# x held by channel in all stages, norms as matmuls on groups of 512 tokens inside the neighbouring loops, convolutions that take both images in turn

## The reference

```python
x = x + g(n0) * einsum(a(n0), b(n0)) @ Wo + bo        # stage 0, n0 = (x - mean) / sqrt(var + eps)
x = x + tokens + sum_e combine_e * (gelu(tokens @ w1[e]) @ w2[e] + b2[e])   # stage 1, 8 experts, top 2
x = x + block_circulant_conv3x3(n2) + b               # stage 2
x = x + moe(n3, gates from graph attention on 262144 edges)                 # stage 3, 4 experts
x = x + proj(linear_attention(q, k, v) + depthwise_conv(v))                 # stage 4
x = x + moe(n5)                                       # stage 5, 8 experts, hidden size 4 times as large
x = x + dynamic_conv(n6, kernel built from the pooled n6)                   # stage 6
x = x + moe(n7)                                       # stage 7, as stage 1
def _layernorm(x, axis=-1, eps=1e-05):
    m = jnp.mean(x, axis=axis, keepdims=True)
    v = jnp.var(x, axis=axis, keepdims=True)
    return (x - m) / jnp.sqrt(v + eps)
```

## Time and profile before

| what | us |
|---|---|
| median of 3 runs | 3209.75 |
| lowest, highest | 3207.09, 3212.43 |
| the profiled execution | 3207.62 |
| its span in the trace | 3205.9 |

### The profile page before, as it was taken

How to read it: one execution, slowest core, us unless ns; L and a number is a source line. 1 busy time by engine, 2 the same in 40 slices (tenths; PEclk the granted TensorE clock), 3 DMA queues, 4 the chain that set the end, 5 groups by cost and what they waited for, 6 DMA issues and landing times.

```text
span 3205.9 us, 20219 instructions
## 1 busy us (share of the span) xinstructions
PE 1521.4 (47%) x6554; PEld 735.1 (23%) x6554; DVE 1561.3 (49%) x2668; ACT 545.2 (17%) x858; POOL 811.7 (25%) x875
## 2 busy tenths in 40 slices
PE   0011113968673000000000012869976999699969
PEld 0011111642232000000000000244464222244443
DVE  8999995365646042222222226464146555520065
ACT  0000001024211000000000002413023555310033
POOL 0000005720003747777777761000000000000000
PEclk6555555558695555555555555869965999799979
DMA  9000001000005101111111100010000000000000
GB/s 399 26 0 0 0 13 35 14 9 0 6 17 11 57 10 18 18 18 18 18 18 18 18 13 2 1 21 1 0 1 3 1 1 1 6 0 1 1 0 27
DMA packets 70842, 65.78 MB, mean 21 GB/s; under 512 B 50449, under 2 KB 64609, under 8 KB 68321
## 3 DMA queue, kind: packets, MB, share of 16 engines
q1 hardware_dynamic: 43712, 54.60, 6.0%
q0 software_dynamic: 27040, 10.02, 3.3%
HBM read 21.96 MB, written 40.50 MB: 19 GB/s over the span
## 4 chain that ended last, share of the span: by engine, by line
PE 42%; DVE 26%; POOL 20%; issue 9%; ACT 2%; DMA 1%; POOLq 0%; DVEq 0%; SPq 0%
POOL rows L1559 15%; PE bank L840 13%; DVE keys L1806 12%; PE bank L516 8%; PE bank L558 7%; POOL rows L1549 2%; POOL tok_end L1564 2%; POOL scratch_start L1541 2%; PE bank L540 2%; DVE n_tok L396 1%; DVE mean L394 1%; PE bank L503 1%; DVE var L403 1%; PE bank L479 1%; DVE n_tok L413 1%
## 5 line engine op out<-in xcount | busy, mean ns | idle before, releaser
L1559 POOL DMA_INDIRECT rows<-scratch_row,idx_ring x512 | 485.8, 949 | 188.8 <-issue 155.7
L750 DVE TENSOR_TENSOR hid<-hid,bank 128x512 f32<-128x512 f32 (+1 forms) x320 | 273.9, 898 | 282.2 <-PE bank L540 281.5
L1222 PE MATMUL bank<-ident,last 128*20 128x128 f32 x3 | 0.8, 409 | 853.2 <-DVEq L1420 853.2
L1806 DVE TENSOR_TENSOR keys<-keys 128x1024 f32<-128x1024 f32 (+1 forms) x388 | 353.6, 953 | 7.5
L516 PE MATMUL bank<-n_chan,weights_odd 64*128 64x512 f32 x896 | 279.0, 710 | 106.6 <-ACT hid L627 106.0
L627 ACT ACTIVATE hid<-bank,weights_odd 128x512 f32<-128x512 f32 x448 | 282.9, 684 | 253.9 <-PE bank L516 253.5
L1678 POOL DMA_INDIRECT keys<-scratch_sorted,weights_odd x128 | 125.3, 979 | 537.4 <-DVEq L1859 495.8
L558 PE MATMUL bank<-hid,weights_odd 128*64 128x512 f32 x896 | 249.2, 638 | 0.5 <-DVE hid L750 0.5
L1709 PE MATMUL bank<-ident,keys 128*128 128x128 f32 x224 | 55.1, 428 | 370.3 <-DVEq L1774 370.3
L840 PE MATMUL bank<-image,diag 128*128 128x512 f32 x512 | 223.5, 595 | 1.2 <-DVE image L812 1.2
L1378 DVE TENSOR_TENSOR keys<-rows,a_dst_e 128x128 f32<-128x128 f32 x18 | 5.5, 307 | 439.3 <-DMA rows<-scratch_row,idx_ring 439.0
(11 more groups left out here) (416 smaller groups left out, 2263.9 us busy)
## 6 DMA issues: line engine op xcount, KB each, us to landing
scratch_sums<-n_tok SPq DMA_DIRECT2D x12, 2048.0 KB, 36.0
rows<-scratch_row,idx_ring POOLq DMA_INDIRECT x576, 2.4
scratch_sums<-sums SPq DMA_DIRECT2D x18, 384.0 KB, 2.3
scratch_start<-n_tok SPq DMA_DIRECT2D x2, 2048.0 KB, 9.0
a_dst_e<-scratch_start SPq DMA_DIRECT2D x1, 4096.0 KB, 13.3
keys<-scratch_sorted,weights_odd POOLq DMA_INDIRECT x136, 2.3
n_chan<-in_x SPq DMA_DIRECT2D x1, 2048.0 KB, 8.1
edge_i<-in_L_ffn_edge_index SPq DMA_DIRECT2D x1, 2048.0 KB, 13.4
```

The source lines that it names most:

```text
L750: v.tensor_tensor(blocks, blocks, bank[4 + b][:, :].unsqueeze(1).broadcast_to([P, KS, 512]), ALU.mult).then_inc(S("scaled"), 1)
L1559: g.indirect_dma_start(out=rows[:, b, c, :], out_offset=None, in_=row_d[:, :], in_offset=at(idx_ring[:, b, c:c + 1])).then_inc(s_gath[b], 16)
L1806: m = v.tensor_tensor(o, p, q, op)
```

## The change

- x stays in `x_pair`, 128 rows (image, channel) by 4096 columns, from the start to the end. `x_tok`, `n_tok`, `n_chan`, `y_pair` and all that turned them go: L462, L479, L568, L828, L550, and the DMA of stage 0.
- The norm works on a group of 512 columns (1024 tokens, both images). TensorE multiplies with `centre`, which subtracts the mean (`ln_centre`); ScalarE copies the result to `n_pair` and squares it (`ln_square`); four matmuls with 32 columns of weights give the variances (`ln_var`); ScalarE takes the root of 128x128 values (`ln_root`), VectorE the reciprocal (`ln_recip`); four matmuls spread it over the channels (`ln_back`); VectorE multiplies (`ln_scale`).
- These steps stand in the loop of the stage before: in stages 1, 3 and 5 two, three and five blocks behind the last down matmul of the group, in stages 2 and 6 between the convolution's groups, after stages 0 and 4 in the loop that makes the output, together with the router of the next stage (`tail_tensor`). Stage 0's own norm stands inside the sort: its reciprocal of 128x1024 values and 8 multiplies are on VectorE between the sort's steps.
- In the mixture loops the gates of all 8 groups are brought in during the first iterations. The sum goes straight to `x_pair`; stages 1 and 7 add `n_pair` in a second VectorE step.
- The convolutions take image 0 and image 1 of a group in turn. VectorE adds lower and upper rows straight to `x_pair`. POOL clears the borders. The copies into the image are made per group (2 on ScalarE, 2 on VectorE) in the loop before; the pooled sums of stage 6 come from one VectorE sum per group in stage 5.
- Stage 4: q, k and v take the two images from the two halves of the rows; turning q and the kv matmuls stand between the convolution's groups; attention, its norm, the projection, the norm of stage 5 and its router form one loop. Stage 0: Wg and Wa are one matmul of 128 output rows (16 instead of 32), and bo is added to x once.

The names below are those of the memory: several tensors share `wide` (n_pair, and the image), `weights_even` and `weights_odd` (weights, and now the squares and roots too). L540 is the spread of the gates before and the down matmul now; L525 is the spread now.

The core of the diff:

```diff
+        def ln_centre(pe, st, n):
+            gap = 4 if st == 0 else 1 if st - 1 in FFN else 2
+            pe.wait_ge(*x_ready(st, n))
+            if n >= gap and st != 0:
+                pe.wait_ge(S("chan"), at(st, "chan") + n - gap + 1)
+            if n == 0 and st - 1 in FFN:
+                pe.wait_ge(S("gate_rows"), at(st - 1, "gate_rows") + 8)
+            if n >= gap and st == 0:
+                pe.wait_ge(S("std"), n - gap + 1)
+            nc.tensor.matmul(ln_bank(st, n)[:, :], centre[:, :], x_pair[:, group(n)], start=True, stop=True).then_inc(S("centred"), 1)
...
+        def ln_square(a, st, n):
+            a.wait_ge(S("centred"), at(st, "centred") + n + 1)
+            dst = tok_mem if st == 0 else n_pair
+            nc.scalar.copy(dst[:, group(n)], ln_bank(st, n)[:, :])
+            nc.scalar.activation(squares[:, n % 2, :], ln_bank(st, n)[:, :], ACT.Square).then_inc(S("squared"), 1)
+        def ln_var(pe, st, n):
+            pe.wait_ge(S("squared"), at(st, "squared") + n + 1)
             for t in range(4):
-                m = nc.tensor.transpose(bank[6 + g % 2][:, t * P:(t + 1) * P], pair_columns(n_tok, 4 * g + t), ident[:, :])
+                m = nc.tensor.matmul(ln_bank(st, n)[32 * t:32 * t + 32, 0:P], averages[:, :], squares[:, n % 2, t * P:(t + 1) * P], start=True, stop=True)
+            m.then_inc(S("var"), 1)
+        def ln_root(a, st, n):
+            r = rstd0[:, n, :] if st == 0 else rstd[:, n % 2, :]
+            a.wait_ge(S("var"), at(st, "var") + n + 1)
+            e = int(st not in MIXERS)
+            nc.scalar.activation(r, ln_bank(st, n)[:, 0:P], ACT.Sqrt, bias=eps[:, e:e + 1]).then_inc(S("std"), 1)
+        def ln_recip(v, st, n):
+            v.wait_ge(S("std"), at(st, "std") + n + 1)
+            v.reciprocal(rstd[:, n % 2, :], rstd[:, n % 2, :]).then_inc(S("rstd"), 1)
+        def ln_back(pe, st, n):
+            r = rstd0[:, n, :] if st == 0 else rstd[:, n % 2, :]
+            pe.wait_ge(S("rstd"), at(st, "rstd") + n + 1)
+            if n >= 4 and st == 0:
+                pe.wait_ge(S("chan"), n - 3)
+            for t in range(4):
+                m = nc.tensor.matmul(ln_bank(st, n)[:, t * P:(t + 1) * P], spread_out[:, t, :], r, start=True, stop=True)
+            m.then_inc(S("rstd_back"), 1)
+        def ln_scale(v, st, n):
+            v.wait_ge(S("rstd_back"), at(st, "rstd_back") + n + 1)
+            dst = (tok_mem if st == 0 else n_pair)[:, group(n)]
+            v.tensor_tensor(dst, ln_bank(st, n)[:, :], dst, ALU.mult).then_inc(S("chan"), 1)
...
+        def tail_tensor(pe, st, k):
+            if 0 <= k - 2 < 8:
+                ln_back(pe, st, k - 2)
+            if 0 <= k - 1 < 8:
+                ln_var(pe, st, k - 1)
+            if 0 <= k < 8:
+                ln_centre(pe, st, k)
+            if 0 <= k - 3 < 8:
+                router_tensor(pe, st, k - 3)
...
-                    pe.wait_ge(S("gate_rows"), at(st, "gate_rows") + 1)
-                if n >= 2:
+                if n >= 1:
                     pe.wait_ge(S("gate_rows"), at(st, "gate_rows") + n)
-                if n >= 3 and st != 7:
-                    pe.wait_ge(S("y_added"), at(st, "y_added") + n - 2)
...
-                    if st == 7:
-                        for t in range(4):
-                            nc.tensor.matmul(bank[6][:, t * P:(t + 1) * P], pair_columns(x_tok, 4 * n + t), ident[:, :], start=(t == 0), stop=False)
...
-            for i in range(SPREAD_LAG, BLOCKS + LAG + 3):
+            for i in range(SPREAD_LAG, BLOCKS + LAG + 5):
                 if i < BLOCKS:
                     up(i)
+                if 1 <= i - SPREAD_LAG <= 6:
+                    gates_in(1 + i - SPREAD_LAG)
...
+                if st != 7:
+                    if behind(i, 5) is not None:
+                        ln_back(pe, st + 1, behind(i, 5))
+                    if behind(i, 3) is not None:
+                        ln_var(pe, st + 1, behind(i, 3))
+                    if behind(i, 2) is not None:
+                        ln_centre(pe, st + 1, behind(i, 2))
...
+                if st != 7:
+                    if behind(i, 3) is not None:
+                        ln_root(a, st + 1, behind(i, 3))
+                    if behind(i, 2) is not None:
+                        ln_square(a, st + 1, behind(i, 2))
+                    if behind(i, 6) is not None and st in (1, 5):
+                        image_scalar(a, st + 1, behind(i, 6))
...
-            def add(n):
-                if st == 7:
-                    return
-                v.wait_ge(S("y_back"), at(st, "y_back") + n + 1)
-                x = x_tok[:, 8 * n:8 * n + 8, :]
-                v.tensor_tensor(x, x, bank[7][:, :].rearrange("p (t c) -> p t c", c=C), ALU.add).then_inc(S("y_added"), 1)
-            for s in range(8 * NS):
+                x = x_pair[:, group(n)]
+                v.tensor_tensor(x, bank[6][:, :], x, ALU.add).then_inc(S("y_ready"), 1)
+                if st in (1, 7):
+                    v.wait_ge(S("y_ready"), at(st, "y_ready") + n + 1)
+                    v.tensor_tensor(x, x, n_pair[:, group(n)], ALU.add).then_inc(S("x_sum"), 1)
...
             for g in range(NT // 4):
-                b, t = divmod(g, 8)
-                pe.wait_ge(S("img"), at(st, "img") + 8 * b + min(8, t + 2))
+                t, b = divmod(g, 2)
+                pe.wait_ge(S("img_low"), at(st, "img_low") + min(8, t + 2))
+                pe.wait_ge(S("img_up"), at(st, "img_up") + min(8, t + 2))
                 if g >= 3:
-                    pe.wait_ge(S("y_ready"), at(st, "y_ready") + g - 2)
-                    pe.wait_ge(S("conv_up"), at(st, "conv_up") + 9 * ((g - 3) // 8) + (g - 3) % 8 + 1)
+                    pe.wait_ge(S("conv_add"), at(st, "conv_add") + 2 * (g - 3) + 2)
                 for n in range(pairs * pairs):
                     px, py = divmod(n, pairs)
                     m = nc.tensor.matmul(bank[g % 3][:, :], weights(b, px, py), window(b, 8 * t, 8, px, py), start=(n == 0), stop=(n == pairs * pairs - 1))
                 m.then_inc(S("conv"), 1)
-                if t == 7:
+                if st != 4:
+                    if b == 0:
+                        if t >= 3:
+                            ln_back(pe, st + 1, t - 3)
+                        if t >= 2:
+                            ln_centre(pe, st + 1, t - 2)
+                    else:
+                        if t >= 2:
+                            ln_var(pe, st + 1, t - 2)
```

1007 lines of the change are left out of this document (522 added, 485 removed).

## The result

| | before | changed |
|---|---|---|
| median, us | 3208.42 | 2996.64 |
| lowest to highest | 3206.22 to 3212.43 | 2987.38 to 3003.76 |
| profiled execution, its span | 3207.62, 3205.9 | 2987.38, 2985.7 |

The ratio is 0.934, with a 95% interval of 0.931 to 0.936: 212 us less. The forecast was 3064 in a range of 2975 to 3130, so the time lies inside the range and the direction was right, but the gain is 212 us where 146 were worked out.

A forecast was written before the change was run, and what follows sets the result against it. TensorE was taken to bound loops and convolutions, VectorE's norm, turning and copies the stretches between, GpSimd's gathers the graph. Terms summed to -146 us from 3207.6, giving 3062, or 3064 as median; range 2975 to 3130.

The forecast's parts named there:

- The two tails: Output, norm and next router behind stages 0 and 4, taken at half clock: +30 us and -27 us.
- rival 1: The clock rises in the new mixed stretches because 512-column centre matmuls stand among short ones: 2981 us, chance 0.17.
- Stage 0's start: From 502.5 to 595.5 us, norm, DMA turn and half of 32 half-clock matmuls go: -60 us.
- The sort's term: Stage 0's norm inside the VectorE-bound sort adds its own duration, reciprocal 6.6 us included: +13 us.
- The loops: Mixture loops gain 2.0 us a group: 0 for stage 1, +1 for stage 3, +16 for stage 5.
- They should be met: In the mixture loops, TensorE's waits for the norm's links should be covered by blocks of 2.8 us between them.
- the cover: In the loops, ScalarE's 4 us and VectorE's 3.2 us more per group stay under TensorE's 13 us.
- Between the stages: Behind the loops of stages 1, 3 and 5 mainly the last group's chain stays: -27, -47 and -30 us.
- The convolutions: Stages 2 and 6 gain +15 and +22 us in the convolutions; the stretches behind lose 14 and 33 us.
- Stage 7: Its loop loses the x-adding matmuls of L550: -9 us.
- Rival 3: A wait for the norm's links halves the clock in every group, 6.55 us for 40 groups: 3326 us, chance 0.06.
- rival 4: Tails worse than half clock: one buffer ring in stage 4 waits 3 us per step, stage 0 likewise: 3112 us, chance 0.12.

## Why the prediction was right, and where it was short

**The two tails** are the step that failed, and the size of the gain with it. The prediction put the group of the tail of stage 0 at 10.4 us at half clock, +30, and the loop of stage 4 at 13.2, -27, because the stretches before had 0.50. They came out at +3.9 and -56.1, with the clock at 0.72 and 0.81. That was rival 1, worked out at 2981 and given a chance of 0.17. So the measured 2996.6 is nearer to rival 1 than to the forecast: it lies in the range because the range took in most of this rival, and outside the forecast's own 3030 to 3095.

In the tail of stage 0 the price itself was right: a round at half clock takes 10.05 us in the run with the earlier multiply (784.11 to 794.16 us). What failed there is the clock alone. In the loop of stage 4 a price failed too: the attention matmuls of a group were put at 3.5 us and take 1.97 at half clock, 12 of the 29 us by which this term missed; the rest goes with the clock, but the run with narrow centre matmuls did not bring this tail back to half clock, so for stage 4 the cause is in part open.

The evidence against rival 1 was the stretch of 54.80 us at 0.50. It was matmuls of 512 columns, but on 64 rows, and the rows were what differed: the run with 64 more rows of zero weights shows it for the g and a matmuls, and the tail with its output matmuls on 128 rows (69.9 us at 0.84) for the tail. The run with narrow centre matmuls shows that the wide matmuls, rival 1's stated cause, had a part in the tail of stage 0 as well (0.52 without them). The rows that would have told were shown already: loops and convolutions at 1.00 use all 128 rows, by two images or two taps at a time. The Trainium skill, "TensorE: Matmul & The Clock Gate", part 1, takes sustained activity for what releases the clock. The clock of 0.50 over the g and a matmuls, busy 20.70 of 20.70 us, shows that a busy engine alone was not enough here.

**Stage 0's start** (-66.9 for -60) had its three parts, norm, DMA turn and half of the 32 matmuls. The 7 us more are the first four of the 16 matmuls, which run at 507.6 us, while VectorE still looks up blocks. The sort's term was right to half a microsecond: the two reciprocal rows and their slope gave 6.6 us for the reciprocal of 128x1024, which took 6.55.

**The loops.** The group's extra was put at 2.0 us and came out at 1.7 in stage 5 (38.9 for 37.2). The single prices were off in both directions: in the timelines four variance matmuls take 0.42 us at full clock, half of the lower bound, the centre matmul 1.10 in the timeline instead of 0.87 (the records of two overlap), spreading back 1.16 as taken. "They should be met" was wrong for one wait: VectorE's multiply stands behind two gate multiplies and came 1.06 us late for the next centre matmul, in every group of stages 1 and 3. The terms 0 and +1 became +4.8 and +2.6. The term of stage 1 also has a slip: 112.8 less 85 is 28 us lost to waits, not 26. Its loop stood at 0.89, which the prediction had named as a sign of being wrong; in the group with VectorE's two graph steps of 4.42 us, and in the one behind it, 21.6 and 17.4 us pass instead of 13.9. The rest of the cover held: ScalarE's room was 3.8 us and the loads cost nothing.

**Between the stages** all three terms were right to 2 us (-27, -47, -30 for -25.1, -46.4, -31.9). For -27 and -30 it was for the stated reason, the chain of the last group. Of -47 the size is in part luck: the parts named, a chain of 8.3 to 11, 19.2 for q, k and v and 13.6 for v, make 41 to 44 us and not 38, and they were taken at half clock, while the stretch of 38.9 us had 0.82 and waits for VectorE. The prediction set the norm's +2.0 a group in the loops against these gains, and this is right; the run with the norm apart shows that the two sides of the move nearly cancel, and that the overlap as such brought nothing here.

**The convolutions** with what follows them were put at +15 - 14 and +22 - 33, and came out 8 and 7 us lower. The gap lies in the convolutions themselves: from the first to the last of their matmuls they take 79.0 us for 73.4 and 238.7 for 229.1, so +5.6 and +9.6. Only five or six of the eight norms stand between the groups, and a variance is cheaper than taken; the stretches behind gave 13 and 28 us, a little less than predicted.

**Stage 7** gained 1.5 and not 9: its groups did shrink, from 11.62 to 10.32 us, but its first sum came 18.5 us after the first gate multiply instead of 13.4, and these 18.5 us stand at 0.67 with TensorE busy throughout; the gates of all groups are brought in there.

**Rival 3**, slower than before, did not come; the slowed reciprocal shows that its mechanism exists, at two thirds of its price, and that its first link had 0.6 us to spare. The ring of stage 4, rival 4, was there (2.86 us in six rounds), hidden in the sum by the better clock and the cheaper attention.
